# Shift products on four row groups, and a new order in the first layer of a two-layer kernel

## The reference

```python
x = x + attn(layernorm(x))      # gated linear attention in chunks of 64, then a gated MLP (352 wide)
x = x + ffn(layernorm(x))       # a graph of six attention nodes
...
for c in range(6):
    q = ew[c, 0] * (nodes[in_q] @ We[eq] + be[eq])      # k and v alike, each from an earlier node
    o = mha(q, k, v, Wq[c], Wk[c], Wv[c], Wo[c])        # 8 heads of 16
    nodes[c] = act_w[c] * o + q
out = layernorm(nodes[5])
```

## Time and profile before

| | us |
|---|---|
| median of three runs | 1185.42 |
| lowest and highest | 1184.21, 1189.61 |
| the profiled execution | 1178.75 |
| its span, first to last instruction | 1176.9 |
| TensorE, VectorE, ScalarE, GpSimd busy | 1117.5, 846.6, 736.3, 429.0 |

### The profile page before, as it was taken

One profiled execution on the slowest core, in us unless ns is written; L12 is line 12 of the kernel. 1 busy time (PEld: TensorE's weight loads), 2 busy tenths in 40 slices (PEclk: granted clock), 3 DMA queues, 4 the chain that ended last, 5 costly groups with the idle time before them and its releaser, 6 DMA issues.

```text
span 1176.9 us, 28120 instructions
## 1 busy us (share of the span) xinstructions
PE 1117.5 (95%) x10295; PEld 774.2 (66%) x10295; DVE 846.6 (72%) x1857; ACT 736.3 (63%) x1595; POOL 429.0 (36%) x848
## 2 busy tenths in 40 slices
PE   8978998878999999999999999999999999999995
PEld 4745555544667777777777777777777777777773
DVE  5567777765777777777777788777777777777783
ACT  3545555542666676667666676767666666766674
POOL 3311111122433333333333378633334333333375
PEclk9999999988999999999999999999999999999998
DMA  8000000005666556666666666756666676666540
GB/s 222 1 1 1 1 0 0 1 1 81 94 93 88 84 85 96 94 85 91 94 92 84 94 94 100 106 85 93 92 92 83 96 93 87 89 95 93 84 70 24
DMA packets 83549, 87.02 MB, mean 74 GB/s; under 512 B 11482, under 2 KB 69342, under 8 KB 83422
## 3 DMA queue, kind: packets, MB, share of 16 engines
q1 hardware_dynamic: 81774, 83.17, 48.5%
q0 software_dynamic: 848, 2.11, 1.1%
q10 hardware_dynamic: 800, 0.05, 0.0%
HBM read 6.51 MB, written 2.10 MB: 7 GB/s over the span
## 4 chain that ended last, share of the span: by engine, by line
PE 79%; DVE 6%; ACT 5%; POOL 5%; issue 3%; DMA 1%; ACTq 0%; DVEq 0%; POOLq 0%
PE bank L1151 71%; PE bank L1497 3%; PE bank L1504 3%; ACT region L629 1%; DVE region L1064 1%; ACT region L636 1%; DVE region L947 1%; PE bank L1470 1%; DVE region L945 1%; POOL out L598 1%; DMA cols<-in_L_attn_gnorm_w 1%; POOL region L427 1%; POOL xall L429 1%; POOL region L425 1%; POOL hl L540 1%
## 5 line engine op out<-in xcount | busy, mean ns | idle before, releaser
L747 ACT ACTIVATE region<-bank 128x512 f32<-128x512 f32 x768 | 416.9, 595 | 262.2 <-PE bank L1151 250.3
L1064 DVE TENSOR_REDUCE region<-bank 128x2 f32<-128x512 f32 x768 | 491.9, 681 | 77.5 <-PE bank L1151 77.3
L1151 PE MATMUL bank<-st 48*128 48x256 f32 x3072 | 375.1, 351 | 5.3 <-DVE region L1064 5.3
L1151 PEld LDWEIGHTS bank<-st 48*128 48x128 f32 x3072 | 266.0, 189 | 84.0 <-issue 30.1
L1151 PE MATMUL bank<-region 128*32 128x256 f32 (+5 forms) x3586 | 253.9, 374 | 4.4 <-DVE region L996 2.7
L540 POOL TENSOR_TENSOR hl<-qk,one_col 128x512 fp32r<-128x512 f32 x96 | 99.8, 1040 | 409.1 <-ACT qk L712 409.1
L1151 PEld LDWEIGHTS bank<-region 128*32 128x32 f32 (+3 forms) x3586 | 127.0, 113 | 94.7 <-issue 26.3
L1151 PE MATMUL bank<-mst,ones 64*128 64x512 bf16 x768 | 150.8, 388 | 0.2 <-ACT region L747 0.2
L543 POOL TENSOR_TENSOR hl<-qk,hl 128x512 fp32r<-128x512 f32 x96 | 122.6, 1278 | 7.5
L1080 DVE COPY mrows<-bank 24x256 bf16<-24x256 bf16 x96 | 26.8, 279 | 98.8 <-PE bank L1470 98.6
L1151 PE MATMUL bank<-region,wgu 128*128 128x512 f32 (+1 forms) x96 | 59.3, 746 | 18.7 <-DVE region L984 17.7
(11 more groups left out here) (195 smaller groups left out, 1452.5 us busy)
## 6 DMA issues: line engine op xcount, KB each, us to landing
st<-hl SPq DMA_DIRECT2D x576, 128.0 KB, 4.5
mst<-mrows SPq DMA_DIRECT2D x192, 6.0 KB
out<-xall POOLq DMA_DIRECT2D x15, 128.0 KB, 3.8
xall<-in_L_attn_hidden_states SPq DMA_DIRECT2D x1, 768.0 KB, 9.1
cst<-in_constants SPq DMA_DIRECT2D x1, 514.5 KB, 4.2
xT<-in_L_ffn_Wq SPq DMA_DIRECT2D x1, 384.0 KB
xT<-in_L_ffn_Wk SPq DMA_DIRECT2D x1, 384.0 KB
xT<-in_L_ffn_Wv SPq DMA_DIRECT2D x1, 384.0 KB
```

Of the source, the lines that this page charges most:

```text
L747: act.activation(to, x_bank(x, k, e)[:, :].rearrange("p (j q) -> p j q", j=2), ACT.Exp).then_inc(B["exp_ok"], 1)
L1064: dve.tensor_reduce(mx[s.n % 2][:, to:to + 2], s_bank(s, k, e)[:, :].rearrange("p (j k) -> p j k", j=2), AX_X, ALU.max, negate=True).then_ ...
L1151: return pe.matmul(o, w, x, start=start, stop=stop, skip_group_check=skip)
```

## The change

1. The maxima are laid out in four blocks of three rows, at partitions 0, 32, 64 and 96, instead of two of 64 rows with zeros; SyncE moves them with four transfers instead of two, and the clearing of `mst` at the start is dropped.
2. The shift products leave `weights` and become `shifts(x, k)`, called in bursts 0 and 2 behind the scores. One call issues four, for the four units of two bursts, each in a row group of 32 and in a bank of its own. So that these two bursts need the same keys and the two pairs of heads, the order of weight units becomes key-major (`kt, g = unit(k)`).
3. Weight units turn through four banks (2, 4, 5, 6). Score units have banks 0 and 1; the very first unit of a step goes to bank 3. Waits are added for that: on the first maximum of the step in `transpose_maxima` and, in the first slots, in `project_qk`; on `vals_ok` in burst 0.
4. In burst 3 the weights come ahead of the scores.
5. First layer, VectorE: Newton steps of tile k, then masks 0 and 1 of tile i, then `silu_gate` 0 and 1, and only then the Newton steps and normalising of tile f. PE: the score products 2 and 3 of tile i come ahead of the `up` products.
6. Draining iterations: ScalarE does `gate_tanh` ahead of the squares of tile k, with the copy of the first steps' queries and keys between; VectorE's gate comes first; GpSimd splits step 0 ahead of `nn`; PE's first scores alternate with `up` and `mlp_out`.
7. Warming products (a matrix of ones times itself, 512 columns) are added: 6 and 4 in the first draining iteration, and two after bursts 1 and 2 of each of the first two node slots.

The core of the diff:

```diff
-S_RING, X_RING = (0, 1, 2), (4, 5, 6)
+S_RING, X_RING = (0, 1), (2, 4, 5, 6)
...
+        def s_turn(s, k, e):
+            return s.n * (UNITS - 1) + 2 * k + e - 1
         def s_bank(s, k, e):
-            return bank[S_RING[(s.n * UNITS + 2 * k + e) % len(S_RING)]]
+            return bank[IN if k == 0 and e == 0 else S_RING[s_turn(s, k, e) % 2]]
         def x_bank(x, k, e):
-            return bank[X_RING[(x.n * UNITS + 2 * k + e) % len(X_RING)]]
+            return bank[X_RING[(2 * k + e) % 4]]
...
                 for e in range(2):
-                    before = s.n * UNITS + 2 * k + e - len(S_RING)
-                    if before >= 0:
-                        pe.wait_ge(B["max_ok"], before + 1)
+                    if k == 0 and e == 0:
+                        if s.n >= 2:
+                            pe.wait_ge(B["vals_ok"], s.n - 1)
+                        else:
+                            pe.wait_ge(B["qk_ok"], s.n + 2)
+                    elif s_turn(s, k, e) >= 2:
+                        n, u = divmod(s_turn(s, k, e) - 2, UNITS - 1)
+                        pe.wait_ge(B["max_ok"], n * UNITS + u + 2)
...
+            def shifts(x, k):
+                if k == 0:
+                    pe.wait_ge(m_in[x.n % 2], 64 * x.uses(2))
+                    if x.n == 0:
+                        pe.wait_ge(A["x1_ok"], ITERS)
+                for g in range(2):
+                    for e in range(2):
+                        before = x.n * UNITS + 2 * (k + g) + e - len(X_RING)
+                        if before >= 0:
+                            pe.wait_ge(B["exp_ok"], before + 1)
+                        rows = slice(32 * (2 * e + g), 32 * (2 * e + g) + MROW)
+                        mm(x_bank(x, k + g, e)[:, :].rearrange("p (j q) -> p j q", j=2), ones[rows, :], mst[x.n % 2][rows, :, :],
+                           stop=False, skip=True)
             def weights(x, k):
-                g, kt = unit(k)
+                kt, g = unit(k)
...
-                for e in range(2):
-                    rows = slice(HALF * e, HALF * e + HALF)
-                    before = x.n * UNITS + 2 * k + e - len(X_RING)
-                    if before >= 0:
-                        pe.wait_ge(B["exp_ok"], before + 1)
-                    mm(x_bank(x, k, e)[:, :].rearrange("p (j q) -> p j q", j=2), ones[rows, :], mst[x.n % 2][rows, 2 * g:2 * g + 2, :], stop=False, skip=True)
...
                 def burst(k):
-                    if s is not None:
+                    if s is not None and k < 3:
                         scores(s, k)
                     if x is not None:
+                        if k % 2 == 0:
+                            shifts(x, k)
                         weights(x, k)
+                    if s is not None and k == 3:
+                        scores(s, k)
...
             first(f, i, k, j), VectorE:
                     newton(dve, ve2, rr2, rt2, k, "r2a", "r2b", "r2c", "rstd2_ok")
+                if i is not None:
+                    scores(i, 0)
+                    scores(i, 1)
+                if j is not None and not draining:
+                    silu_gate(j, 0)
+                    silu_gate(j, 1)
                 if f is not None:
                     newton(dve, ve, rr, rt, f, "ra", "rb", "rc", "rstd1_ok")
...
             first(f, i, k, j), PE:
+                if i is not None:
+                    for t in range(2, TPI):
+                        pe.wait_ge(A["am_ok"], TPI * i + t - 1)
+                        heads_scores(i, t)
                 if j is not None:
```

More of the change, by code:

```diff
@@ L525, in first @@
                     pool.tensor_tensor(xn, hh, xs.unsqueeze(2).to_broadcast([P, TPI, D]), ALU.mult).then_inc(A["xn_ok"], 1)
+                if f is None and i is None and k is not None:
+                    split(stages(0)[1])
                 if k is not None:
@@ L551, in split_maxima @@
                 pool.wait_ge(B["max_ok"], m.n * UNITS + UNITS)
[L552 to L555, removed]
+                flat = mx[m.n % 2].rearrange("p (a j) -> p a j", j=2)
+                rest = mrest.rearrange("p (a j) -> p a j", j=2)
+                hi, mid, low = (mxp[m.n % 2][:, :, i, :] for i in range(MROW))
+                one = one_col[:, :].unsqueeze(2).to_broadcast([P, KT * 4, 2])
                 pool.tensor_tensor(hi, flat, one, ALU.mult).then_inc(B["mhi_ok"], 1)
@@ L605, in _ @@
             pool.wait_ge(L["ln_in"], 32)
-            for t in range(EARLY):
+            for t in range(1, EARLY):
                 phase(*stages(t))
@@ L632, in first @@
                     act.activation(keT, bank[2][:, 0:TPI * QK].rearrange("p (t k) -> p t k", t=TPI), ACT.Copy).then_inc(A["keT_ok"], 1)
+                draining = f is None and i is None
+                if draining:
+                    gate_tanh(j, 0)
+                    if k is not None:
+                        phase(*stages(0))
+                    gate_tanh(j, 1)
+                    if k is None:
+                        phase(*stages(2))
                 if k is not None:
@@ L847, in first @@
                     dve.tensor_scalar(ve[:, 1, :], mv[:, 1, :], 1.0 + RMS_EPS, RMS_EPS * LN_EPS, ALU.mult, ALU.add).then_inc(A["ve_ok"].sem, 1)
+                draining = f is None and i is None
+                if draining:
+                    silu_gate(j, 0)
+                    silu_gate(j, 1)
+                    if k is None:
+                        maxes(stages(2)[2], 0)
+                    times_up(j, 0)
+                    times_up(j, 1)
+                    if k is None:
+                        maxes(stages(2)[2], 1)
                 if k is not None:
@@ L1224, in first @@
                     transpose_n(k)
+                if i is not None:
+                    for t in range(2, TPI):
+                        pe.wait_ge(A["am_ok"], TPI * i + t - 1)
+                        heads_scores(i, t)
                 if j is not None:
-                    if f is None and i is None and k is None:
+                    last = f is None and i is None and k is None
+                    if last:
                         scores(stages(2)[2], 0)
-                        scores(stages(2)[2], 1)
                         project_qk(stages(2)[1])
@@ L1232, in first @@
                         up(j, m)
+                    if last:
+                        scores(stages(2)[2], 1)
                     pe.wait_ge(A["hid_ok"], j * MT + 1)
@@ L1239, in first @@
                     project_qk(stages(1)[1])
-                if i is not None:
-                    for t in range(2, TPI):
-                        pe.wait_ge(A["am_ok"], TPI * i + t - 1)
-                        heads_scores(i, t)
                 if f is not None:
@@ L1251, in first @@
                 if j is not None:
-                    if f is None and i is None and k is None:
+                    if last:
                         scores(stages(2)[2], 2)
+                    mlp_out(j)
+                    if last:
                         scores(stages(2)[2], 3)
-                    mlp_out(j)
                     if f is None and i is None:
@@ L1298, in first @@
                     fold_transposes(1)
+                if f is None and i is not None:
+                    warm(6, 3)
                 if i is not None:
@@ L1306, in first @@
                     n.then_inc(A["b_ps"], 1)
+                if f is None and j is not None:
+                    warm(4, 3)
                 if j is not None:
```

42 lines of the change are left out of this document (20 added, 22 removed).

## The result

The changed kernel takes 1197.95 us at the median of six runs (1192.28 to 1205.19). The kernel before took 1185.26 us beside it. The ratio is 1.0106, with an interval of 1.0067 to 1.0145: slower by 1.1%. The forecast was 1175 us and faster; the end of its range was 1197. The likeliest case, its sign and, by a microsecond, its range were wrong. The profiled execution took 1196.71 us, 18.0 more than that of before.

The account below looks back on a forecast made before the run. TensorE's own queue was taken to bound node slots, VectorE's order to stall TensorE in the first layer. Profiled 1178.75 + 13.5 - 24 = 1168.3 us, plus 6.7 to the median: 1175 us, range 1124 to 1197.

Parts of the forecast that it names:

- likeliest case: Whole kernel: seams paid in the node steps, first layer gains; median 1175 us, faster; chance 0.58.
- seam: Bursts 0 and 2: switching between 64-row and 32-row groups costs 0.12 us into the shift set, 0.20 us back.
- three rivals: Seams free, 1127 us, chance 0.22; four groups taking turns, 1218 us, 0.08; first layer gives little, 1191 us, 0.12.
- node part: Node steps: +0.16 us a slot, times 94 +15 us, less 1.5 in the last node's slots; +13.5 us.
- two pairs removed: Bursts 1 and 3: their shift pairs go, 2 x 0.23 us, -0.46 us a slot.
- two sets with seams: Bursts 0 and 2: four shifts cost 0.54 us where a pair cost 0.23; rounded to +0.60 us a slot.
- burst 2's wait for its banks: Burst 2: with two score banks, its scores need both maxima of burst 1; +0.07 us a slot.
- context wait covered: After burst 2: its extra 0.3 us covers TensorE's wait for VectorE's normalised context; -0.05 us a slot.
- wait of `project` for the context copy: Behind burst 3: ScalarE's copy of the node waits for the projection anyway; nothing added.
- The reductions allow 2.18 plus some 0.06 for the signal: Burst 1 to burst 2: reductions plus signal allow the start later than TensorE's 2.17 us arrival; +0.07 us.
- Bank 3 [...] free: Node slots: bank 3, shared with the first scores unit, costs nothing, its maximum being read while pv runs (1.93 us).
- rebuilt order of the forecast: Full first-layer iterations: score products fill TensorE's gap, next transposes at 213.1 us instead of 216.5; 3.1 us taken, five times.

Follow-up runs that it names:

- layer part: Kernel before with only the first layer's reorderings, draining order and that part's warming products; 1161.35 us, ratio 0.9799.
- the kernel with three rows: Kernel before with each shift product taking three rows instead of 64, in a 32-row group, still in pairs; 1287.02 us, ratio 1.0862.
- node part alone: Kernel before with only the node steps' changes and the warming between bursts of the first node slots; 1226.48 us, ratio 1.0346.
- second profile: The changed kernel run and profiled once more, unedited, against the kernel before; 1199.74 us, ratio 1.0120.
- layer part, old first tile: The layer part with VectorE's old order kept for tile 0, against the kernel before; 1154.74 us, ratio 0.9727.

## Why the prediction was wrong, point by point

**What was right.** The layer part: -24 forecast, -23.9 measured by the medians, iterations of 27.0 us against 27.2. The seam: 0.34 us from the end of the scores to the end of the set, 0.34 forecast; from there to the first weight pair 602.67 - 602.36 = 0.31, 0.31 forecast. Its cause is shown by the kernel with three rows, and that four groups work side by side by the equal length of pair and set. The Trainium skill (TensorEngine Tiling (Array Packing), Tiling Modes, Key Properties) says that a change of tiling mode drains TensorE. These runs agree for 64-row and 32-row groups too: such a change costs time, 0.27 to 0.29 us there and back. So none of the three rivals took place.

**What failed is the size of the node part**: +13.5 us by the sum, +37 (changed kernel less layer part) to +41 (node part alone) by the medians. A slot by its own terms:

| term | forecast | measured |
|---|---|---|
| two pairs removed | -0.46 | -0.46 |
| two sets with seams | +0.60 | +0.58 |
| burst 2's wait for its banks | +0.07 | +0.16 |
| context wait covered | -0.05 | -0.05 |
| wait of `project` for the context copy | 0 ("waits for the projection anyway") | +0.04 |
| slot | +0.16 | +0.27 (9.25 - 8.99 = 0.26) |

The first step to fail is the sentence "The reductions allow 2.18 plus some 0.06 for the signal". The interval of 2.18 us was right (604.67 to 606.85). But from the end of a reduction to the start of the scores that need its bank it is 0.15 us, not 0.06. The prediction names no row for the 0.06. The trace before has such a delay at another wait, that of the weight load for VectorE's context (609.67 to 609.73), and for scores behind a reduction it has 0.15: the first of these four, 0.68 us each, ends at 286.32, and the scores of rows 9 start at 286.47.

```profile
285.64 2.62 DVE L1064 TENSOR_REDUCE region<-bank 128x2 f32<-128x512 f32 x4
...
609.25 0.42 DVE L1090 TENSOR_TENSOR region<-bank,region 128x256 f32<-128x256 f32 x1
...
609.73 0.20 PEld L1504 LDWEIGHTS bank<-cst,region 128*128 128x128 f32 x2 [0.18 <-DVE region L1090]
```

So the price could have been read before the run, at the same pair of operations. The second step is the copy on ScalarE: I had asked whether it delays the exponentials, not whether the shorter burst 3 uncovers it. The two make 0.13 us a slot; the sets came out 0.02 us cheaper, so a slot is 0.10 to 0.11 us dearer than forecast: +10 us over 94.

**The first slots were priced at nothing beyond that.** They take 6.8 us (or 9.5, in the second profile) more than before, 3.1 of it the steady price. The rest is partly this: in two of the first slots the last tiles of the first layer are transposed into bank 3, which is now also the bank of a first scores unit, and TensorE waits for its maximum:

```profile
PE bank L1353 <- DVE region L1079: 2.7, 2, 1.4
```

I had checked bank 3 for a steady slot, where pv covers it, and not for the slots with these transposes. "Bank 3 [...] free" is wrong there. The remaining 1 to 4 us may be stretches at reduced clock, whose place changes between executions; this was not taken apart.

**The clock was not in the sum.** Every run, profiled or not, has its mean granted clock. Time times clock is what the run would take if the lower level were never granted and all of it were TensorE's work; the rest is what the clock took:

| kernel, median run | time | clock | time x clock | rest |
|---|---|---|---|---|
| before | 1185.3 | 0.972 | 1152 | 33 |
| layer part | 1161.4 | 0.985 | 1144 | 17 |
| node part | 1226.5 | 0.9625 | 1180 | 46 |
| changed | 1199.7 | 0.979 | 1174 | 25 |
| changed, its fastest and slowest run | 1190.8, 1205.2 | 0.985, 0.973 | 1173, 1173 | 18, 32 |
| layer part, old first tile | 1154.7 | 0.990 | 1143 | 12 |

The ten runs of the changed kernel lie up to 14.4 us apart; in the fourth column all ten lie between 1172.7 and 1176.4, so nearly all of its spread is the clock. (Waits don't stretch with the clock: the profiled execution of before gives 1156 in that column and its median 1152, so it is good to some 4 us.) It also splits the parts. By it the node part costs 28 us of work (0.26 x 94 = 24.4, and the early slots) and 13 us of clock. Beside the layer part it is 30 and 8. The layer part, which I sized by its waits and hit, is 8 us of work and 16 of clock. In the kernel before each iteration had one stretch of 3.4 us at the lower level (granted clock 0.94 in rows 2), from 209.8 us on in this one, right behind the wait of 2.61 us that is gone. The eight products behind that wait took 5.40 us, at a granted clock of 0.68, and now take 3.87 at 1.00. TensorE's idle time in an iteration fell by 1.78 us (30.33 - 26.84 to 27.00 - 25.29). Together that is the 3.3 us by which an iteration is shorter. The rebuilt order of the forecast gave these products 3.8 us (208.6 to 212.4), so it had the full clock in it without saying so or giving a reason. That it came true is luck in this respect. And the forecast added the 6.7 us between profiled execution and median as a constant, when most of that too goes with the clock: the profiled execution of before ran at 0.981, the median at 0.972. One slip in its range changes nothing: two seams at half their price take away 0.16 x 188 = 30 us, not 25.

With the slots put right (+0.26 x 94 = +24.4), the last node's -1.5, the first slots' +4 and the layer's -24, the sum would be 1178.75 + 2.9 + 6.7 = 1188 us: no change that can be told. The 10 us from there to the measured median are the clock that the node part costs beside the layer part (8), and 2 us that I can't place. The trace of before could not give them.

**What stays open.** Why the clock falls at one place in one execution and not in the next of the same kernel (the stretch at 1156.7 us above). Whether the reduction's 0.15 us is all signal, since the reductions were not shortened. Whether a seam is the array running empty or weights that can no longer be loaded ahead: no run parts the two. And why the node part, whose code comes later, goes with more time at the lower clock in the first layer.

## What to carry to other kernels

Packing small products into smaller row groups bought only what it removed less two seams: here two pairs of 0.23 us a slot against two sets that cost 0.29 us more each. A slot got shorter (8.91 us for 8.99) only where the set stood beside a change of shape that is paid already, and waits appeared where something had run under the time that was saved. For each shortened stretch, list what else ran beneath it (reductions, copies), with the delay from release to start read at a real wait of the same two operations, before the saving is counted. A new order that serves one stage should not be applied in the iterations of a pipeline where this stage is absent, and the runs' clocks are to be read beside their times, since half of a gain or more may lie there (16 of 24 us for the layer part).

## What the runs showed of the hardware that was not expected

- Products on 32-row groups between products on 64-row groups cost 0.27 to 0.29 us a set, whether it has two products or four (10.07 against 8.99 us a slot with four such pairs).
- From the end of a VectorE reduction to the start of the TensorE product that waits for it: 0.15 us (606.85 to 607.00). Behind VectorE's context product the weight load starts after 0.06 us (609.67 to 609.73 in the kernel before).
- Three waits of TensorE of 2.81 us together, with the products between them short, were followed by 10.2 us at the lower clock (33.3 to 43.5 us). At 44.59 us TensorE was at a product that it had reached at 37.13 in the kernel before, 7.5 us later; 5.2 of them are left at the first residual.
- In the first iteration of the changed order (one execution each), small VectorE operations took up to twice as long where they ran behind the masks: the Newton steps at 26.24 and 26.55 us took 0.27 and 0.31 us, and 0.17 each in the kernel before. What ran beside them was not isolated.
